# Two 64-row column strips per tile in the experts of a two-layer kernel

## The chip, the cores and the metric

The kernel runs on one core of one Trainium2 chip. The metric is the time of one execution on the device, in microseconds (us); the kernel before takes 3040.6 us, the median of three runs (3038.39 to 3043.71).

Engines are named as in the profile: PE is TensorE's matmul, PEld its weight load, DVE is VectorE, ACT is ScalarE, POOL is GpSimd, SP is SyncE. A "q" behind the name (ACTq, SPq) is the sequencer of that engine, which here issues DMAs.

## The reference

Two layers, each a sequence mixer and a mixture of experts, on 4 x 512 = 2048 tokens of width 512. The change touches the experts of the second layer ("layer 1" in the code). What it computes, cut to what matters:

```python
T, H, E, K, I = 2048, 512, 32, 8, 256
logits = x @ router_w; scores = sigmoid(logits)
# 4 of 8 groups of experts are kept per token, then the best 8 experts
tkw = take_along_axis(scores, top_k_index); tkw = tkw / tkw.sum(-1) * 2.5
flat_idx = top_k_index.reshape(-1); sort_idx = argsort(flat_idx)
xs = repeat(x, K)[sort_idx]                      # 16384 rows, sorted by expert
group_sizes = bincount(flat_idx, length=E)
gate = ragged_dot(xs, w_gate, group_sizes)       # [512 x 256] of each expert
up   = ragged_dot(xs, w_up,   group_sizes)       # [512 x 256]
down = ragged_dot(silu(gate) * up, w_down, group_sizes)   # [256 x 512]
routed = (down[unsort] * tkw).sum(axis=1)        # 8 rows added up per token
out = routed + shared(x)                         # everything in float32
```

## The kernel before

The router stage of layer 1 (`route_stage`, here called with L == 1) counts the rows of each expert, rounds each count up to whole tiles of P = 128 rows, and gives each pair of token and expert a slot in a table in HBM, `slots_in` (`xs1`). It writes each token's normalised row into its 8 slots with indirect DMAs from POOL (line 880), together with a record: the 8 weights, the 8 slot numbers and the token's number. It also writes which expert each tile belongs to (`tile_expert`), and after how many tiles each expert begins (`ends`). The table is zeroed in advance, during the attention stage; a slot that no token took gives a zero row, whose result goes to a spare row of the output.

How many tiles there are is fixed when the program is built, for the worst routing: NTILE1 = (16384 + 32 x 127) // 128 = 159. Tiles past the last expert's rows are computed all the same, with expert 31's weights.

`expert_stage1` then runs over the 159 tiles. It is written for each engine by hand, with semaphores between them, and every engine takes its work in a fixed order:

- **PE**, in round t: `turn_hidden(t-1)` (two 128-column transposes of the hidden rows, tile `e_psh`, line 2032), `up(t)` (four matmuls with the tile's 128 transposed rows as the stationary side and 512 columns of gate and up weights as the moving side, `e_psg`, line 2025), `down(t-1)` (two such matmuls into `e_pso`, line 2041). Each float32 matmul stands in the profile as two MATMUL rows, so `up` is eight rows and `down` four.
- **ACT**: `gate(t)` (SiLU of the gate half, `e_sg`, line 1896), then in two of every four rounds `reload` (one load of records, or four loads of rows, for tiles some rounds ahead, lines 1913 and 1908), then `empty(t-1)` (the result times the row's weight, `e_yo`, line 1903), which waits for `down(t-1)`.
- **DVE**: transposes the rows of tile t+1 (`e_xsT`, line 1960), copies the turned hidden rows of tile t-1 (`e_hT`, line 1965), multiplies gate by up (`e_h`, line 1970), and with four short operations works out the weight and the target row of each slot (`e_mine`, `e_pad`, `e_wrow`, `e_dest`).
- **POOL**: `add(t)`, one indirect DMA per tile that adds the 128 result rows into the output (line 1877). Two such adds must not touch the same row at once. Rows of one expert are of different tokens, so adds of one expert may be in flight together: tiles go by turns to two lanes, each with a semaphore of its own. An add always waits until the one before it in its lane has landed, and where the expert changes it waits for the tile just before it too (the table `after` holds that count). Eight result buffers (OUT = 8) lie between ACT and POOL.
- **SP**: `refill` loads one expert's weights (1.5 MB in three DMAs) into a ring of four, as soon as the expert three before it is done; `announce` tells PE that an expert's weights are there.

Layer 0's experts, which the change doesn't touch, have 64 rows each. They already run two experts side by side: one in the left 64 columns of the PE array, one in the right 64 (`tile_position`, lines 1681 and 1700).

## Time and profile before

| | us |
|---|---|
| median of three runs | 3040.6 |
| the profiled execution | 3042.4 |
| its span, first to last instruction | 3040.7 |
| first matmul of layer 1's experts | 2166.0 |
| last start of an `up` matmul | 3023.6 |
| end of the last result written by ACT (`e_yo`) | 3029.5 |
| last add issued | 3031.2 |

The stage of layer 1's experts is the last of the program, about 875 us of 3041. In the profiled execution PE is busy for 88% of the span, DVE for 48%, POOL for 37%, ACT for 25%; the mean granted clock of PE is 0.956 of full speed. A group of rows gives the line, engine, operation and tiles, the count, the busy time, the mean of one in ns, and behind the last bar how long the engine was idle just before these instructions and what ended the idle time. The 192 ns weight loads of PEld run beside matmuls. A MATMUL row's duration is longer than its share of the engine, since matmuls are pipelined: the spacing of their starts tells what one costs.

### The profile page before, as it was taken

The page shows a single profiled execution, that of the slowest core. Times are in us where ns is not written, and L with a number is a line of the kernel's source. Part 1 is how long each engine was busy: PE and PEld are TensorE (multiplying, and loading weights), DVE is VectorE, ACT ScalarE, POOL GpSimd, SP SyncE. Part 2 cuts the span into 40 slices and gives each one's busy share as a digit, 9 for nine tenths or more (in the row PEclk, how much of TensorE's full clock was granted, in tenths as well). Part 3 has the DMA queues.
Part 4 walks back from the last instruction along what each step waited for, and adds up shares of the span by engine and source line. Part 5 has one row for each costly group of instructions (what it writes and reads, how often), then busy time and mean ns, then how long its engine had stood idle before and what let it go on. Part 6 is the DMA issues. An engine that isn't in the chain of part 4 may idle for free. (4 is left out here: it accounts for less than half of the span.)

```text
span 3040.7 us, 33280 instructions
## 1 busy us (share of the span) xinstructions
PE 2672.1 (88%) x8935; PEld 1175.4 (39%) x8936; DVE 1459.8 (48%) x2609; ACT 773.9 (25%) x1190; POOL 1121.2 (37%) x803
## 2 busy tenths in 40 slices
PE   5888975799999887588999998994499999999998
PEld 2343432344444343233333333441244444444443
DVE  7999999532010033155666564620244444444443
ACT  4747554110000010033333342100011211111111
POOL 2777656233100041126555632257322222232222
PEclk8999999999999999789999998997799999999999
DMA  3333322310300399780177001345677867887765
GB/s 127 112 100 108 81 65 68 115 57 14 117 0 14 116 342 339 247 223 27 41 198 199 12 1 49 133 172 210 159 167 154 179 125 145 181 187 158 157 98 71
DMA packets 364039, 385.31 MB, mean 127 GB/s; under 512 B 69666, under 2 KB 268643, under 8 KB 363938
## 3 DMA queue, kind: packets, MB, share of 16 engines
q1 hardware_dynamic: 212962, 243.49, 25.9%
q0 software_dynamic: 45376, 97.18, 15.4%
q10 hardware_dynamic: 105600, 43.35, 7.2%
q8 instruction: 56, 0.92, 0.1%
q14 instruction: 45, 0.37, 0.0%
HBM read 236.15 MB, written 160.53 MB: 130 GB/s over the span
## 5 line engine op out<-in xcount | busy, mean ns | idle before, releaser
L2025 PE MATMUL e_psg<-e_wgu,e_xsT 128*128 x1272 | 575.0, 595 | 80.5 <-DVE e_xsT L1960 80.5
L1877 POOL DMA_INDIRECT out_x<-e_yo,e_dest x159 | 246.7, 1551 | 629.1 <-DMA out_x<-e_yo,e_dest 343.6
L285 POOL TENSOR_TENSOR hc<-hs,bcst 128x1024 f32<-128x1024 f32 x128 | 300.8, 2350 | 176.6 <-DVE ps_b L505 170.0
L2025 PEld LDWEIGHTS e_psg<-e_wgu,e_xsT 128*128 128x128 f32 x1272 | 231.3, 192 | 311.1 <-issue 311.1
L630 PE MATMUL ps_y<-hc,ident 128*128 128x512 f32 x512 | 241.3, 609 | 90.2 <-POOL hc L285 89.9
L1970 DVE TENSOR_TENSOR e_h<-e_psg,e_sg 128x256 f32<-128x256 f32 x159 | 67.6, 425 | 496.1 <-ACT e_sg L1896 490.1
L2041 PE MATMUL e_pso<-e_wd,e_hT 128*128 x636 | 298.9, 592 | 0.7 <-ACT e_yo L1903 0.7
L511 DVE TENSOR_TENSOR_SCAN hs<-dA,ps_b 128x1024 f32<-128x1024 f32 x128 | 292.6, 2286 | 6.6 <-ACT dA L415 2.4
L1233 PE MATMUL r_ps_t<-r_wd,r_h 128*128 128x512 f32 x480 | 209.6, 597 | 8.5 <-DVE r_h L982 4.3
L1896 ACT ACTIVATE e_sg<-e_psg 128x256 f32<-128x256 f32 x159 | 61.1, 384 | 530.5 <-PE e_psg L2025 530.5
L982 DVE TENSOR_TENSOR r_h<-r_ps_u,r_sg 128x512 f32<-128x512 f32 x60 | 41.4, 691 | 318.1 <-PE r_ps_u L1214 308.8
L415 ACT ACTIVATE dA<-dt,a_neg 128x511 f32<-128x511 f32 x256 | 165.5, 713 | 111.0 <-DVE hs L511 105.9
L2629 DVE TENSOR_REDUCE a_nm<-a_ps 128x2 f32<-128x992 f32 x128 | 146.1, 1185 | 88.7 <-PE a_ps L2873 88.4
L630 PEld LDWEIGHTS ps_y<-hc,ident 128*128 128x128 f32 x512 | 92.8, 191 | 233.2 <-POOL hc L285 138.2
L1960 DVE STREAM_TRANSPOSE e_xsT<-e_xs 128x512 f32<-128x512 f32 x159 | 175.4, 1104 | 11.2 <-DMA e_xs<-slots_in 6.7
L2041 PEld LDWEIGHTS e_pso<-e_wd,e_hT 128*128 128x128 f32 x636 | 120.8, 190 | 152.5 <-issue 152.5
L880 POOL DMA_INDIRECT slots_in<-r_xn,scat x128 | 126.4, 987 | 135.7 <-DMA slots_in<-r_xn,scat 55.0
L1903 ACT ACTIVATE e_yo<-e_pso,e_wrow 128x512 f32<-128x512 f32 x159 | 109.3, 688 | 260.9 <-PE e_pso L2041 172.0
L2391 ACT ACTIVATE a_pt<-a_ps 128x1024 f32<-128x1024 f32 (+1 forms) x128 | 126.2, 1022 | 188.4 <-PE a_ps L2890 127.6
L915 ACT ACTIVATE r_sg<-r_ps_g 128x512 f32<-128x512 f32 x60 | 35.8, 597 | 522.9 <-PE r_ps_g L1214 522.9
L505 DVE TENSOR_TENSOR ps_b<-du,bcst 128x1024 f32<-128x1024 f32 x128 | 159.4, 1246 | 8.4 <-DVE hs L511 0.5
L1214 PE MATMUL r_ps_g<-r_xnT,r_wgu 128*128 128x512 f32 x352 | 158.6, 593 | 0.0
(415 smaller groups left out, 3492.6 us busy)
## 6 DMA issues: line engine op xcount, KB each, us to landing
slots_in<-zeros SPq DMA_DIRECT2D x160, 256.0 KB, 2.3
e_xs<-slots_in ACTq DMA_DIRECT2D x160, 256.0 KB
bcst<-bc_rows SPq DMA_DIRECT2D x128, 256.0 KB, 4.4
e_wgu<-in_wg SPq DMA_DIRECT2D x32, 512.0 KB
e_wgu<-in_wu SPq DMA_DIRECT2D x32, 512.0 KB
e_wd<-in_wd SPq DMA_DIRECT2D x32, 512.0 KB
e_w<-in_wg SPq DMA_DIRECT2D x11, 1408.0 KB
e_w<-in_wu SPq DMA_DIRECT2D x11, 1408.0 KB
```

The costliest lines, as they stand in the source:

```text
L285: pool.tensor_tensor(hc[:, it % 2, half(h), :], hs[:, it % 2, half(h), :], bc(bcst[:, q, 1, :], 1, HB), ALU.mult).then_inc(sem["hc"], 1)
L415: i = act.activation(dA[:, it % 2, t, 1:], dt[:, b % 2, t, 1:], ACT.Exp, scale=a_neg[:, n, t:t + 1])
L505: dve.tensor_tensor(ps_b[:, :, :], du[:, b % 2, half(h), :], bc(bcst[:, q, 0, :], 1, HB), ALU.mult)\
L511: dve.tensor_tensor_scan(hs[:, it % 2, half(h), :].rearrange(flat), dA[:, it % 2, half(h), :].rearrange(flat), ps_b[:, :, :].rearrange(fla ...
L630: i = pe.matmul(ps_y[:, t, :], c["ident"][:, :], hc[:, it % 2, t, :], start=False, stop=False, skip_group_check=True)
L1214: i = pe.matmul(ps[:, f % 2, :], w[:, k, f * P:(f + 1) * P], xnT[:, b, k, :], start=k == 0, stop=k == KH - 1)
L1233: i = pe.matmul(ps_t[:, j % 2, :], h[:, f, j * P:(j + 1) * P], wd[:, f, :], start=f == 0, stop=f == FC - 1)
L1877: pool.indirect_dma_start(out[:, :], bass.IndirectOffsetOnAxis(dest[:, q, 0:1], 0), yo[:, q, :], None, bounds_check=T + 2 * P - 1, oob_is_ ...
L1960: dve.transpose(xsT[:, q % 2, :, :].rearrange("p k (s j) -> p k s j", j=DQ), xs[:, q // RING % 2, part, :].rearrange("p s (i k) -> p k s i ...
L2025: j = pe.matmul(ps_g[:, q % 2, :], xsT[:, q % 2, k, :], wgu[:, bass.ds(e % RING, 1), k, :], start=k == 0, stop=k == KH - 1)
L2041: j = pe.matmul(ps_o[:, q % 2, :], hT[:, q % 2, a, :], wd[:, bass.ds(e % RING, 1), a, :], start=a == 0, stop=a == NW - 1)
L2629: dve.tensor_reduce(nm[:, i % 8, 2 * z:2 * z + 2], ps[:, at:at + 2, 0:S2], AX_X, ALU.max, negate=True)\
```

## The change

Counts are rounded up to HALF = 64 rows per expert instead of 128. A tile still has 128 rows, but is now two strips of 64 rows, and its second strip can belong to another expert than the first. The worst case is 287 strips, so NTILE1 becomes 144.

- **PE** runs each of `up`'s and `down`'s matmuls as two: rows 0 to 63 in the left 64 columns of the array, rows 64 to 127 in the right. The left strip's weights are read from the ring `e_wgu`, `e_wd`, the right strip's from copies, `e_cgu` and `e_cd`. The transposes of the hidden rows stay as they are, over 128 columns.
- **The copies**: ACT copies the second strip's gate and up weights (128 x 2048 float32, 1 MB) for tile t+2 at the end of each round; DVE copies its down weights (128 x 1024) for tile t+1 at the end of each round, after a wait for `down(t-1)`. Both first load the strip's expert number and wait until it is announced. They copy whether or not the two strips have the same expert.
- **POOL** issues two adds per tile, one per strip; the lanes are now the strips. Strip s of tile t waits for strip s of tile t-1 to have landed, and, where the expert changes, for the strip just before it.
- **ACT** also loads the token numbers a second time, into `e_token`, laid out by strips (64 x 8 x 2 words), behind each load of records.
- **SP** announces expert e+3 right behind the refill that loads it, and refills the next only after that.
- In the router, the table of experts is by strips (three columns instead of two), and `ends` is worked out later, as half the strips, rounded up.

```diff
+HALF = P // 2
+NHALF1 = (T * K1 + E * (HALF - 1)) // HALF
+NTILE1 = (NHALF1 + 1) // 2
+NSLOT1 = NTILE1 * P
...
             @block.sync
...
+                for s in range(AHEAD):
+                    announce(s, 0)
                 with sp.Fori(0, E // RING - 1) as i:
                     for q in range(RING):
-                        announce(q, i)
                         refill(i * RING + q, q)
+                        announce((q + AHEAD) % RING, i + (1 if q > 0 else 0))
...
             @block.gpsimd
...
+                    for s in range(2):
...
+                        if before is not None:
+                            hold(pool, out_of[1 - s], before, c["held"])
+                        if not head:
+                            hold(pool, out_of[s], landed_before, c["held"])
...
+                        pool.indirect_dma_start(out[:, :], bass.IndirectOffsetOnAxis(dest[:, q, s:s + 1], 0), yo[half(s), q, :], None,
...
             @block.scalar
...
+                    act.dma_start(token[:, r, :, :], D["xs1"][bass.ds(row0, RING * P), H + 2 * K1:H + RECW + 1]
+                                  .rearrange("(v p) w -> p v w", p=HALF)).then_inc(rec_in[r], 16)
+
+                def copied(t, q):
+
+                    e = act.value_load(ids[0:1, bass.ds(2 * t + 1, 1)], min_val=0, max_val=E - 1)
+                    hold(act, sem["ready"], 1 + e + 1, c["held"])
+                    act.activation(cgu[:, q % 2, :, :], wgu[:, bass.ds(e % RING, 1), :, :].rearrange("p o k n -> p (o k) n"),
+                                   ACT.Copy).then_inc(sem["cgu"], 1)
...
                         gate(i * OUT + q, q)
                         reload(i * OUT + q, q)
                         empty(i * OUT + q - 1, q + OUT - 1)
+                        copied(i * OUT + q + 2, q)
...
             @block.vector
...
+                def copied(t, q):
+
+                    e = dve.value_load(ids[0:1, bass.ds(2 * t + 1, 1)], min_val=0, max_val=E - 1)
+                    hold(dve, sem["ready"], 1 + e + 1, c["held"])
+                    if not (isinstance(t, int) and t < 2):
+                        dve.wait_ge(sem["down"], 1 + t - 1)
+                    dve.tensor_copy(cd[:, q % 2, :, :], wd[:, bass.ds(e % RING, 1), :, :].rearrange("p o k n -> p (o k) n"))\
+                       .then_inc(sem["cd"], 1)
...
                         product(t, q)
                         addressed(t, q, i + 1)
+                        if not (last and q == REST - 1):
+                            copied(t + 1, q + 1)
...
             @block.tensor
...
                     pe.wait_ge(sem["xsT"], 1 + t + 1)
+                    pe.wait_ge(sem["cgu"], 1 + t + 1)
                     for k in range(KH):
-                        j = pe.matmul(ps_g[:, q % 2, :], xsT[:, q % 2, k, :], wgu[:, bass.ds(e % RING, 1), k, :],
-                                      start=k == 0, stop=k == KH - 1)
+                        for s in range(2):
+                            w = cgu[:, q % 2, k, :] if s else wgu[:, bass.ds(e % RING, 1), k, :]
+                            j = pe.matmul(ps_g[half(s), q % 2, :], xsT[:, q % 2, k, half(s)], w, start=k == 0, stop=k == KH - 1,
+                                          tile_position=(0, s * HALF), skip_group_check=True)
```

On PE, one round in the steady loop: the transposes (`e_psh`), `up` (`e_psg`) and the start of `down` (`e_pso`). Before:

```order
L2032 MATMUL e_psh<-ident,e_h 128x128 x2
L2023 REGISTER_ALU
L2025 ISA
L2025 MATMUL e_psg<-e_wgu,e_xsT 128x512
L2025 ISA
L2025 MATMUL e_psg<-e_wgu,e_xsT 128x512
L2025 ISA
L2025 MATMUL e_psg<-e_wgu,e_xsT 128x512
L2025 ISA
L2025 MATMUL e_psg<-e_wgu,e_xsT 128x512
L2036 TENSOR_LOAD e_ids
```

The same place on PE with the change:

```order
L2077 MATMUL e_psh<-ident,e_h 128x128 x2
L2070 ISA
L2070 MATMUL e_psg<-e_wgu,e_xsT 64x512
L2070 MATMUL e_psg<-e_cgu,e_xsT 64x512
L2070 ISA
L2070 MATMUL e_psg<-e_wgu,e_xsT 64x512
L2070 MATMUL e_psg<-e_cgu,e_xsT 64x512
L2070 ISA
L2070 MATMUL e_psg<-e_wgu,e_xsT 64x512
L2070 MATMUL e_psg<-e_cgu,e_xsT 64x512
L2070 ISA
```

Each matmul over 128 rows has become a pair over 64, between transposes that still span 128.

On ACT, the start of the stage: the loads of rows (`e_xs`) and records (`e_rec`) and the first SiLU. Before:

```order
L1908 DMA e_xs<-slots_in 32x16x128 x4
L1913 DMA e_rec<-slots_in 128x4x17
L1908 DMA e_xs<-slots_in 32x16x128 x4
L1913 DMA e_rec<-slots_in 128x4x17
L1896 ACTIVATE e_sg<-e_psg 128x256 x2
```

The same place on ACT with the change:

```order
L1919 DMA e_xs<-slots_in 32x16x128 x4
L1924 DMA e_rec<-slots_in 128x4x17
L1926 DMA e_token<-slots_in 64x8x2
L1919 DMA e_xs<-slots_in 32x16x128 x4
L1924 DMA e_rec<-slots_in 128x4x17
L1926 DMA e_token<-slots_in 64x8x2
L1931 TENSOR_LOAD e_ids
L1931 ISA x2
L75 REGISTER_ALU
L1933 ISA
L1933 ACTIVATE e_cgu<-e_wgu 128x2048
```

Two token loads and then the first weight copy, for which PE's first `up` waits, stand ahead of the first SiLU.

On POOL, the adds of the steady loop. Before, one per tile:

```order
L1871 ISA
L1871 TENSOR_LOAD e_after
L1871 ISA x2
L1877 DMA out_x<-e_yo,e_dest 2304x512
L73 REGISTER_ALU
L1871 ISA
```

The same place on POOL with the change, one tile:

```order
L1881 TENSOR_LOAD e_after
L1881 ISA x2
L75 REGISTER_ALU
L1888 DMA out_x<-e_yo,e_dest 2304x512
L1881 ISA
L1881 TENSOR_LOAD e_after
L1881 ISA x2
L1888 DMA out_x<-e_yo,e_dest 2304x512
```

The second add has a load of its own from `after`, and waits of its own.

## Rows read from the trace of the kernel before

**Rows 1.** The page, groups of layer 1's `up` and adds:
```profile
L2025 PE MATMUL e_psg<-e_wgu,e_xsT 128*128 x1272 | 575.0, 595 | 80.5 <-DVE e_xsT L1960 80.5
L1877 POOL DMA_INDIRECT out_x<-e_yo,e_dest x159 | 246.7, 1551 | 629.1 <-DMA out_x<-e_yo,e_dest 343.6
```

**Rows 2.** Busy time by stretch; columns PE, PEld, DVE, ACT, POOL, clock, DMA share, GB/s:
```profile
2400.00:2600.00 200.00, 200.00 (x522) 93.54 (x521) 82.46 (x261) 40.35 (x75) 57.36 (x37) 1.00 0.76 142
```

**Rows 3.** Timeline, one round in steady state; start, duration, instruction, [idle before <-releaser]:
```profile
2603.87 3.60 PE L2025 MATMUL e_psg<-e_wgu,e_xsT 128*128 x8
...
2607.51 0.38 ACT L1896 ACTIVATE e_sg<-e_psg 128x256 f32<-128x256 f32 x1 [2.84 <-PE e_psg L2025]
...
2607.92 0.42 DVE L1970 TENSOR_TENSOR e_h<-e_psg,e_sg 128x256 f32<-128x256 f32 x1 [3.04 <-ACT e_sg L1896]
...
2609.25 3.60 PE L2025 MATMUL e_psg<-e_wgu,e_xsT 128*128 x8
2609.36 0.69 ACT L1903 ACTIVATE e_yo<-e_pso,e_wrow 128x512 f32<-128x512 f32 x1 [1.47 <-PE e_pso L2041]
```

**Rows 4.** Timeline of layer 0's strips, weight loads of `down` in pairs:
```profile
1128.37 0.14 PEld L1700 LDWEIGHTS e_pso<-e_w,e_hT 128*64 128x64 f32 x2 [0.28 <-issue]
1128.80 0.14 PEld L1700 LDWEIGHTS e_pso<-e_w,e_hT 96*64 96x64 f32 x2 [0.28 <-issue]
```

**Rows 5.** Timeline, layer 0, from 64-column matmuls to 128-column transposes:
```profile
1139.39 0.49 PE L1681 MATMUL e_psu<-e_w,e_xsT 128*64 128x352 f32 x2
1139.81 0.39 PE L1668 MATMUL e_psx<-ident,r_wgu 128*128 128x128 f32 x1
```

**Rows 6.** The transposes of layer 0, all 60: duration ns min/median/max:
```profile
L1668 PE MATMUL e_psx<-ident,r_wgu x60: 283/285/387, 1067.9 to 1255.8; 128*128 128x128 f32 x60
```

**Rows 7.** Timeline, layer 0, from 128-column transposes to 64-column matmuls and their loads:
```profile
1123.22 0.75 PE L1668 MATMUL e_psx<-ident,r_wgu 128*128 128x128 f32 x4
1123.90 1.07 PE L1720 MATMUL e_psa<-x_resid 128*64 128x512 f32 x2
...
1124.38 0.14 PEld L1720 LDWEIGHTS e_psa<-x_resid 128*64 128x64 f32 x1 [0.29 <-issue]
1124.81 0.14 PEld L1720 LDWEIGHTS e_psa<-x_resid 128*64 128x64 f32 x1 [0.29 <-issue]
```

**Rows 8.** ACT groups, from SBUF to SBUF, of two sizes:
```profile
L365 ACT ACTIVATE w<-w 128x512 f32<-128x512 f32 x16 | 9.5, 627 | 6.0 <-DVE e L467 6.0
L2381 ACT ACTIVATE a_sd<-a_sd 128x1024 f32<-128x1024 f32 x4 | 4.2, 1057 | 4.2 <-DVEq L2559 4.2
```

**Rows 9.** Timeline, start of the stage:
```profile
2156.16 2.02 ACTq L1908 DMA_DIRECT2D e_xs<-slots_in  x4
...
2164.09 3.63 ACTq L1913 DMA_DIRECT2D e_rec<-slots_in  x1
...
2166.05 6.33 PE L2025 MATMUL e_psg<-e_wgu,e_xsT 128*128 x8 [80.53 <-DVE e_xsT L1960]
```

**Rows 10.** ACT timeline, the four loads of rows in two rounds:
```profile
2182.75 2.14 ACTq L1908 DMA_DIRECT2D e_xs<-slots_in  x4
...
2785.27 4.68 ACTq L1908 DMA_DIRECT2D e_xs<-slots_in  x4
```

**Rows 11.** POOL timeline, adds at two changes of expert:
```profile
2186.68 1.58 POOL L1877 DMA_INDIRECT out_x<-e_yo,e_dest  x1 [4.45 <-ACT e_yo L1903]
2196.91 1.55 POOL L1877 DMA_INDIRECT out_x<-e_yo,e_dest  x1 [8.65 <-issue]
...
2857.46 1.55 POOL L1877 DMA_INDIRECT out_x<-e_yo,e_dest  x1 [6.66 <-issue]
2863.42 1.55 POOL L1877 DMA_INDIRECT out_x<-e_yo,e_dest  x1 [4.41 <-issue]
```

**Rows 12.** The chain of waits near the end, where no weights load: issue to landing:
```profile
3001.46 4.71 DMA out_x<-e_yo,e_dest
```

**Rows 13.** POOL's scatter of the router, another indirect DMA:
```profile
L880 POOL DMA_INDIRECT slots_in<-r_xn,scat x128 | 126.4, 987 | 135.7 <-DMA slots_in<-r_xn,scat 55.0 <-DVE r_xn L1032 45.6 <-issue 35.1
```

More of the change, by code:

```diff
@@ L125, in constants @@
         idx_i = own("idx_i", [P, E], I32)
-        tile_i = own("tile_i", [P, 2], I32)
+        tile_i = own("tile_i", [P, 3], I32)
         @block.gpsimd
@@ L1128, in _ @@
                     first_slots(base1)
-                    for a in range(2):
+                    for a in range(3):
                         step(dve.tensor_scalar(past[:, :], tcum[:, :], c["tile_no"][:, a:a + 1], None, ALU.is_le))
                         step(dve.tensor_reduce(te[:, a:a + 1], past[:, :], AX_X, ALU.add))
+                    step(dve.tensor_scalar(tf[0:1, :], tcum[0:1, :], 1.0, None, ALU.add))
+                    step(dve.tensor_copy(ti[0:1, :], tf[0:1, :]))
+                    step(dve.tensor_scalar(route["ends"][0:1, 1:], ti[0:1, :], 1, None, ALU.arith_shift_right), wait=False)
                     step(dve.tensor_scalar(te[:, :], te[:, :], float(E - 1), None, ALU.min))
@@ L1804, in expert_stage1 @@
         spare1 = pl.sb("e1_spare1", [P, 2])
-        apart = pl.sb("e1_apart", [1, NTILE1], I32)
-        after_i = pl.sb("e1_afteri", [1, NTILE1 + 1], I32)
-        after = pl.sb("e1_after", [1, NTILE1], I32)
+        apart = pl.sb("e1_apart", [1, 2 * NTILE1], I32)
+        after_i = pl.sb("e1_afteri", [1, 2 * NTILE1], I32)
+        after = pl.sb("e1_after", [1, 2 * NTILE1], I32)
+        token = pl.sb("e1_token", [HALF, 2, RING * 2, 2])
         mine = pl.sb("e1_mine", [P, 2, K1])
         wrow = pl.sb("e1_wrow", [P, OUT, 1])
-        pad = pl.sb("e1_pad", [P, 2, 1])
-        dest = pl.sb("e1_dest", [P, OUT, 1], I32)
+        pad = pl.sb("e1_pad", [HALF, 2, 2])
+        dest = pl.sb("e1_dest", [HALF, OUT, 2], I32)
         ps_g = pl.ps("e1_psg", [P, 2, 512])
@@ L1816, in expert_stage1 @@
                                               "htr", "hT", "down", "yo", "added", "preset", "iota", "named", "chosen", "dest",
-                                              "apart", "after")}
+                                              "apart", "after", "cgu", "cd")}
         landed = [sem[f"w{s}"] for s in range(RING)]
@@ L1861, in _ @@
                 pool.wait_ge(sem["after"], 1 + 1)
                 def add(t, q, turn):
-                    same = 8 * OUT * turn + 16 * (q // 2)
-                    head = isinstance(turn, int) and turn == 0
+                    head = isinstance(turn, int) and turn == 0 and q == 0
+                    landed_before = 16 * OUT * turn + 16 * q
                     hold(pool, sem["yo"], 1 + t + 1, c["held"])
-                    if head and q < 3:
-                        before = 16 if q > 0 else None
-                    else:
-                        before = pool.value_load(after[0:1, bass.ds(t, 1)], min_val=16, max_val=16 * NTILE1)
@@ L1872, in add @@
-                    if before is not None:
-                        hold(pool, out_of[1 - q % 2], before, c["held"])
-                    if not (head and q < 2):
-                        hold(pool, out_of[q % 2], same, c["held"])
-                        pool.sem_inc(sem["added"], 1)
-                    pool.indirect_dma_start(out[:, :], bass.IndirectOffsetOnAxis(dest[:, q, 0:1], 0), yo[:, q, :], None,
-                                            bounds_check=T + 2 * P - 1, oob_is_err=True, compute_op=ALU.add)\
-                        .then_inc(out_of[q % 2], 16)
+                    for s in range(2):
+                        if head and s == 0:
+                            before = None
+                        elif (head and s == 1) or (isinstance(turn, int) and turn == 0 and q == 1 and s == 0):
+                            before = 16
+                        else:
+                            before = pool.value_load(after[0:1, bass.ds(2 * t + s, 1)], min_val=16, max_val=16 * NTILE1)
+                        if before is not None:
+                            hold(pool, out_of[1 - s], before, c["held"])
+                        if not head:
+                            hold(pool, out_of[s], landed_before, c["held"])
+                            if s == 1:
+                                pool.sem_inc(sem["added"], 1)
+                        pool.indirect_dma_start(out[:, :], bass.IndirectOffsetOnAxis(dest[:, q, s:s + 1], 0), yo[half(s), q, :], None,
+                                                bounds_check=T + 2 * P - 1, oob_is_err=True, compute_op=ALU.add)\
+                            .then_inc(out_of[s], 16)
@@ L1985, in addressed @@
                     dve.tensor_reduce(wrow[:, q, :], mine[:, q % 2, :], AX_X, ALU.add).then_inc(sem["chosen"], 1)
[L1986 removed]
+                    dve.scalar_tensor_tensor(out=dest[:, q, :], in0=pad[:, q % 2, :], scalar=-1.0, in1=word,
                                              op0=ALU.add, op1=ALU.add).then_inc(sem["dest"], 1)
@@ L2040, in down @@
                     for a in range(NW):
-                        j = pe.matmul(ps_o[:, q % 2, :], hT[:, q % 2, a, :], wd[:, bass.ds(e % RING, 1), a, :],
-                                      start=a == 0, stop=a == NW - 1)
+                        for s in range(2):
+                            w = cd[:, q % 2, a, :] if s else wd[:, bass.ds(e % RING, 1), a, :]
+                            j = pe.matmul(ps_o[half(s), q % 2, :], hT[:, q % 2, a, half(s)], w, start=a == 0, stop=a == NW - 1,
+                                          tile_position=(0, s * HALF), skip_group_check=True)
                     j.then_inc(sem["down"], 1)
```

73 lines of the change are left out of this document (40 added, 33 removed).

## The prediction

> **What bounds the kernel now.** I read the page first, then the busy time by stretch, then the timeline of one round, and last POOL's adds. Layer 1's experts are the last 875 us, and there PE is the bound: it waits once, 80.5 us, before the stage's first matmul [rows 1], and in a stretch of 200 us it is busy for 200.00 us at the full granted clock (1.00, the 2.4 GHz level) [rows 2]. One round, from `up` to `up`, takes 2609.25 - 2603.87 = 5.38 us [rows 3]. It holds 12 MATMUL rows of 512 columns and two transposes; 159 rounds are 855 us, which is the stage. ACT and DVE are idle for more than half of each round. POOL is not: its 159 adds are busy for 246.7 us and wait for 629.1, over half of it for earlier adds to land [rows 1]. It keeps up, but it is the engine nearest to PE.
>
> **Fewer tiles.** 15 rounds of 5.38 us go: -80.7 us.
>
> **Strips on PE.** Layer 0's experts show what a pair of 64-column matmuls costs. Their weight loads come in pairs, and the pairs stand 1128.80 - 1128.37 = 0.43 us apart [rows 4], for 512 columns. Twelve times 0.43 is 5.16, which leaves 0.22 of a 5.38 us round for two transposes, 0.11 each: so 0.43 is also what one 128-column matmul costs today. Two strips cost what one full matmul costs, and their two loads (0.14 us) fit beside it. Nothing is added there.
>
> What is added is the turn from one width to the other, twice per round: the transposes stay 128 wide. Layer 0 shows both. From 64 to 128: the last pair starts at 1139.39 to 1139.42 and streams 352 columns, 0.43 x 352 / 512 = 0.29 us, so the next could start at 1139.71; it starts at 1139.81, 0.10 late [rows 5], and this first transpose lasts 0.39 us where the median of 60 is 0.285, another 0.10 [rows 5, 6]. From 128 to 64: four transposes span 0.75 us from 1123.22, so the last starts at 1123.22 + 0.75 - 0.285 = 1123.685, and the next matmul 0.215 later instead of the 0.11 that a transpose takes: 0.11 late. The pair after the next is loaded at 1124.38, 0.48 after 1123.90 where 0.43 is the rule (1124.81 - 1124.38): another 0.05 [rows 7]. Sum: 0.20 + 0.16 = 0.36 us per round, so a round takes 5.74 us, and 144 x 0.36 = +51.8 us. The ends: if only the late starts count, 0.21 per round, +30; nothing at all if `up`'s first load could slip in early, +0. No row speaks for more than 0.36. I take 0.36, since both parts are there in one and the same handover.
>
> The Trainium skill, "TensorEngine Tiling (Array Packing)", Key Properties, says that a change of tiling mode drains TensorE. The trace agrees, with the 0.20 and 0.16 us above. Who goes only by that page's promise of independent tiles would leave the 51.8 us out and expect about 2970 us.
>
> **ACT's copy.** SBUF to SBUF, 128x512 takes 627 ns and 128x1024 takes 1057 [rows 8]: 430 ns per 512 columns, so 128x2048 takes 627 + 3 x 430 = 1917 ns. In a plain round `e_yo` starts 2609.36 - 2607.51 = 1.85 us after `e_sg` and ends at 2.54 [rows 3]. Then come the load of the expert's number, a wait that is met, and the copy. What number and waits cost before the engine starts is not shown for ACT; POOL does the like between the last `e_yo` (3029.5) and the last add (3031.2), 1.7 us, and zero is the other end. The copy ends at 4.5 to 6.2 us. The next `e_sg` is due at 5.74, and PE needs its product later still: `e_h` ends at 2608.34 and PE's transposes start at 2609.25 - 0.22 = 2609.03, a cover of 0.7 us [rows 3]. So a plain round is free. In one round of four the loads of rows hold ACT for 2.14 us first [rows 10], `e_yo` ends near 3.1 and the copy at 5.0 to 6.7: at most 0.3 late beyond the cover, 36 x 0.3 = 11 us, at least nothing. Once in a while these loads take 4.68 us [rows 10]; then the copy ends near 8 and PE loses about 2 us. I take +3 us in all, range 0 to 11. Behind the copy on ACT stand the next SiLU and the next loads; DVE and PE wait for the SiLU.
>
> **DVE's copy** of 128x1024 waits for `down(t-1)`, which ends when `e_yo` starts, at 1.85. ACT's 1057 ns for the same size is the nearest row. With the row transposes (1.1) and the hidden copy (0.4) behind it, which are queued behind this wait, DVE is done at 4.4; `down` needs the hidden rows at about 5.4, and the next product begins at 6.1. Hidden; a copy twice as long would just still be.
>
> **Start of the stage.** PE's first `up` now waits for the first copy, which stands behind ten loads of before and two new ones. ACT was done with its loads at 2164.09 + 3.63 = 2167.72, and PE started at 2166.05 [rows 9]. A new token load costs between 0.5 (a load of rows here, 2.02 / 4) and 3.6 us (the record load just before, when the queue is full) [rows 9]; one of each kind gives 4.1, the copy 1.9 more: 2167.7 + 4.1 + 1.9 = 2173.7 at worst, 2170.6 with both loads cheap. +4.6 to +7.7; I take +6. The later copies have a whole slow first `up` (6.33 us) as cover.
>
> **Weights.** `ready` is now announced before it is needed by two tiles more, and SP holds each refill until the one before it has landed. With the reference's routing the experts take 273 strips; in its tightest place (expert 16, 3 strips) expert 19 must land within two rounds, 11.5 us, for 1.5 MB. Once, 0 to 5 us: +1.
>
> **Router, zeroing, end.** Three more short DVE operations come after the first slots are out and beside 128 scatters of POOL; fewer slots are zeroed in a stretch where the DMA queues idle: 0. At the end two half adds stand for one: one more issue, less to land: 0, range -1 to +2.
>
> **Sum** against the profiled execution, 3042.4: -80.7 + 51.8 + 3 + 6 + 1 = -18.9, so 3023.5. The median of before is 1.8 under its profiled execution: **3022 us**.
>
> **The rivals.**
>
> *A, the chain of adds becomes the bound (slower).* Today's add has two rounds, 10.8 us, from its issue to the next in its lane. After the change each lane has one add per round, 5.74 us. A quiet full add lands in 4.71 us [rows 12], and where the next waits for it, it goes out after 2863.42 - 2857.46 = 5.96; a busy one, with weights on their way, after 10.23 [rows 11]. A half add should be shorter: its issue perhaps 0.99 us, as the router's scatter, instead of 1.55 [rows 1, 13], and some of the transfer goes. Bounds for the quiet cycle: 5.96 - 0.56 = 5.4 if only the issue shrinks, (5.96 - 0.56) / 2 = 2.7 if all the rest halves; I take 4.5. Busy: 9.7 to 4.8, I take 7.9. How many adds are busy no row tells; with 28% as an estimate, a lane needs 0.72 x 4.5 + 0.28 x 7.9 = 5.45 us on average: just under 5.74. Of the 31 changes of expert 12 fall inside a tile, by that same routing, and put its second strip some 4 us back, 48 us in all; the result buffers let POOL fall seven rounds behind, 40 us, and the spare 0.29 us per round gives back 42 over the stage. So it holds. At the full add's figures the mean is 0.72 x 5.4 + 0.28 x 9.7 = 6.6: 0.86 us more than PE per round, over the 118 rounds with weights on their way 101 us, plus 48, less the 40 in the buffers: +109, some 3131 us. At a mean of 6.0, nearer to my figures, it is 31 + 48 - 40 = +39: **3061 us**. The point from which it decides is a mean cycle of about 5.7 us. Against it: nothing in today's POOL rows shows it falling behind for more than one add; for it: over half of its waits are for landings already.
>
> *B, ACT becomes the bound.* If numbers, waits and copy take 1.5 us more than taken, every fourth round is 1.2 us longer than the cover allows, 36 x 1.2 = +43, and plain rounds lose a little: 3066 us, slower too. Against it: ACT has only 0.38 + 0.69 us of work per round today.
>
> *C, the turns of width are hidden.* Then -51.8 falls off: 2970 us. Against it: both handovers of layer 0 show the delay, in both halves.
>
> **How the numbers follow.** Forecast 0.60 (its own range 3008 to 3035), A 0.22, B 0.08, C 0.10. A measurement of this kernel tells 0.2% from no change, 6 us: faster is below 3034.5. The forecast's upper edge and mild cases of A and B lie within 0.2% either way: same 0.08. Faster 0.67, slower 0.25. For 8 in 10 the range leaves out the deeper half of C and the dear half of A: 2985 to 3070.
>
> **What would show it.** PE rows of `up` and `down`: 144 x 16 and 144 x 8, pairs 0.43 us apart; the first transpose of a round near 0.39 us, the rest 0.28; a round of 5.74 us. PE's wait before the first `up` some 86 us and for ACT's copy. POOL adds x288 near 1 us each; their start stays within about 20 us of `e_yo`'s end if the forecast is right. If A is right, ACT's `e_yo` waits for POOL's adds in groups, and PE for `e_yo`. If B is right, PE's transposes wait for `e_h` behind copies on ACT. A round of 5.4 us would be C. The prediction is wrong if a half add's landing isn't shorter than a full one's, or if the copy takes much over 2 us.

## The result: 3080 us, slower by 38

The changed kernel takes 3079.95 us (3074.26 to 3085.48), the kernel before beside it 3042.15 us (3038.39 to 3047.17): a ratio of 1.0123, 95% interval 1.0096 to 1.0150. The forecast was 3022 us. Among the experiments, one execution of chain32 (3674 us) and one of apart_out (3615 us) ran at a clearly lower granted clock, 0.81 and 0.735, and the ratios leave these two out.

Of the profiled execution (span 3083.8 us), the chain of waits by line and four groups of the page:

```profile
DMA out_x<-e_yo,e_dest 22%; POOLq L1881 1%; PE e_psg L2070 0%; ACTq L1919 0%; POOL out_x L1888 0%; POOLq L76 0%; POOLq L1888 0%; POOLq L75 0%; ACTq L1926 0%; ACT e_yo L1914 0%; ACT e_cgu L1933 0%; PE e_pso L2089 0%; ACTq L1924 0%; POOLq L1887 0%; POOLq L1894 0%
...
L1888 POOL DMA_INDIRECT out_x<-e_yo,e_dest x288 | 424.9, 1475 | 489.9 <-DMA out_x<-e_yo,e_dest 262.4
L2070 PE MATMUL e_psg<-e_wgu,e_xsT 128*64 x1152 | 529.0, 602 | 80.9 <-ACT e_cgu L1933 80.9
...
L1933 ACT ACTIVATE e_cgu<-e_wgu 128x2048 f32 x144 | 275.2, 1912 | 133.2 <-issue 131.2
...
L2007 DVE COPY e_cd<-e_wd 128x1024 f32 x144 | 105.6, 733 | 132.0 <-PE e_pso L2089 84.6
```

The chain that ended last no longer runs through PE's matmuls: 22% of the span is the landing of adds, where in the kernel before 27% were PE's matmuls. Busy time by stretch, columns as in [rows 2], and one round of PE's timeline:

```profile
2250.00:2400.00 150.00, 150.00 (x684) 50.96 (x682) 79.01 (x210) 77.99 (x79) 72.53 (x49) 1.00 0.71 146
2400.00:2600.00 200.00, 194.47 (x866) 64.36 (x864) 99.00 (x264) 98.55 (x100) 96.05 (x65) 0.98 0.67 136
2600.00:2800.00 200.00, 179.82 (x792) 59.03 (x788) 91.08 (x245) 89.97 (x92) 88.09 (x60) 0.97 0.70 150
```

```profile
2602.63 0.64 PE L2070 MATMUL e_psg<-e_wgu,e_xsT 128*64 x1
...
2607.93 0.50 PE L2077 MATMUL e_psh<-ident,e_h 128*128 128x128 f32 x2
2608.37 0.64 PE L2070 MATMUL e_psg<-e_wgu,e_xsT 128*64 x1
```

A round that nothing holds up takes 5.74 us, as forecast. Up to 2400 us PE is busy throughout, as in [rows 2]; after that it loses 6 and then 20 us in 200. Who waits, between 2400 and 3000 us (in total, times, longest):

```profile
POOL out_x L1888 <- DMA out_x<-e_yo,e_dest: 168.0, 77, 5.8
...
DVE e_mine L2018 <- POOLq L1887: 74.2, 44, 10.8
...
PE e_pso L2089 <- DVE e_hT L1994: 33.3, 19, 8.6
```

POOL waits for adds to land. DVE, which may fill a buffer's addresses only after that buffer's add of eight tiles ago has landed (`added`, L1887), stands for POOL in `e_mine`; the hidden rows' copy `e_hT` stands behind it on DVE, and PE waits for that. How far POOL is behind shows in the counts of a stretch that begins with the stage and ends at 2500 us:

```profile
L1888 POOL DMA_INDIRECT out_x<-e_yo,e_dest x96 | 142.3, 1483 | 195.5 <-DMA out_x<-e_yo,e_dest 103.2 <-issue 53.4 <-ACT e_yo L1914 39.0
L1914 ACT ACTIVATE e_yo<-e_pso,e_wrow 128x512 f32<-128x512 f32 x53 | 36.4, 687 | 89.5 <-PE e_pso L2089 68.6 <-issue 8.7 <-DVE e_dest L2025 6.7
```

96 half adds are 48 tiles, of 53 finished ones. In the kernel before the same stretch has 60 of each.

**Where the 43 us between the two profiled spans went.** Four moments of the changed kernel's timeline: the first load of rows, the first and the last SiLU, the last add.

```profile
2160.63 2.65 ACTq L1919 DMA_DIRECT2D e_xs<-slots_in  x4
...
2183.49 0.38 ACT L1907 ACTIVATE e_sg<-e_psg 128x256 f32<-128x256 f32 x1 [4.62 <-PE e_psg L2070]
...
3050.91 0.38 ACT L1907 ACTIVATE e_sg<-e_psg 128x256 f32<-128x256 f32 x1 [3.33 <-PE e_psg L2070]
...
3075.08 1.42 POOL L1888 DMA_INDIRECT out_x<-e_yo,e_dest  x1 [1.20 <-DMA out_x<-e_yo,e_dest]
```

and of the kernel before, the first and last SiLU (its first load is in [rows 9]):

```profile
2172.41 0.38 ACT L1896 ACTIVATE e_sg<-e_psg 128x256 f32<-128x256 f32 x1 [104.55 <-PE e_psg L2025]
...
3024.24 0.38 ACT L1896 ACTIVATE e_sg<-e_psg 128x256 f32<-128x256 f32 x1 [2.97 <-PE e_psg L2025]
```

- The stage begins 2160.63 - 2156.16 = 4.5 us later. No reading speaks for the change as the cause: the experiments, most of them with its router, begin the stage anywhere from 2149 to 2159 us. So below I give the **stage's length** too, from the first load of rows to the end of the span: 884.5 us before, 923.2 after.
- First load to first SiLU: 16.25 us before, 22.86 after, +6.6.
- First to last SiLU: before 851.8 us, of which 158 x 5.38 = 850.0; after 867.4 us, of which 143 x 5.74 = 820.8. The rounds give 29.2 us back, and 46.6 - 1.8 = 44.8 us are stalls.
- Last SiLU to the end: 16.5 us before, 32.9 after, +16.4: POOL still has its backlog to add.

Sum: 4.5 + 6.6 - 29.2 + 44.8 + 16.4 = 43.1 us.

### The profile page after: what moved, and what is told of

Read it like the earlier page. It is cut to its first block and busy times, and to the rows that moved or that the text cites. A ratio compares the mean times of both kernels' runs of the same rounds, so it can differ in the third digit from the quotient of the medians.

```text
span 3083.8 us, 39087 instructions
## 1 busy us (share of the span) xinstructions
PE 2665.0 (86%) x10451; PEld 1058.0 (34%) x10454; DVE 1541.4 (50%) x2653; ACT 1032.3 (33%) x1305; POOL 1298.6 (42%) x932
## 5 line engine op out<-in xcount | busy, mean ns | idle before, releaser
L1888 POOL DMA_INDIRECT out_x<-e_yo,e_dest x288 | 424.9, 1475 | 489.9 <-DMA out_x<-e_yo,e_dest 262.4
L2070 PE MATMUL e_psg<-e_wgu,e_xsT 128*64 x1152 | 529.0, 602 | 80.9 <-ACT e_cgu L1933 80.9
L2070 PE MATMUL e_psg<-e_cgu,e_xsT 128*64 128x512 f32 x1152 | 529.0, 602 | 0.0
L1933 ACT ACTIVATE e_cgu<-e_wgu 128x2048 f32 x144 | 275.2, 1912 | 133.2 <-issue 131.2
L2089 PE MATMUL e_pso<-e_wd,e_hT 128*64 x576 | 278.1, 606 | 34.2 <-DVE e_hT L1994 34.0
L2089 PE MATMUL e_pso<-e_cd,e_hT 128*64 128x512 f32 x576 | 278.3, 606 | 0.0
L2070 PEld LDWEIGHTS e_psg<-e_wgu,e_xsT 128*64 128x64 f32 x1152 | 146.9, 137 | 349.1 <-issue 332.2
L1914 ACT ACTIVATE e_yo<-e_pso,e_wrow 128x512 f32<-128x512 f32 x144 | 99.0, 687 | 277.5 <-PE e_pso L2089 205.9
L2007 DVE COPY e_cd<-e_wd 128x1024 f32 x144 | 105.6, 733 | 132.0 <-PE e_pso L2089 84.6
L1989 DVE STREAM_TRANSPOSE e_xsT<-e_xs 128x512 f32<-128x512 f32 x144 | 167.6, 1164 | 6.5 <-DMA e_xs<-slots_in 6.5
```

Of the source, the lines that this page charges most:

```text
L1888: pool.indirect_dma_start(out[:, :], bass.IndirectOffsetOnAxis(dest[:, q, s:s + 1], 0), yo[half(s), q, :], None, bounds_check=T + 2 * P - ...
L1933: act.activation(cgu[:, q % 2, :, :], wgu[:, bass.ds(e % RING, 1), :, :].rearrange("p o k n -> p (o k) n"), ACT.Copy).then_inc(sem["cgu"], 1)
L1989: dve.transpose(xsT[:, q % 2, :, :].rearrange("p k (s j) -> p k s j", j=DQ), xs[:, q // RING % 2, part, :].rearrange("p s (i k) -> p k s i ...
L2070: j = pe.matmul(ps_g[half(s), q % 2, :], xsT[:, q % 2, k, half(s)], w, start=k == 0, stop=k == KH - 1, tile_position=(0, s * HALF), skip_g ...
L2089: j = pe.matmul(ps_o[half(s), q % 2, :], hT[:, q % 2, a, half(s)], w, start=a == 0, stop=a == NW - 1, tile_position=(0, s * HALF), skip_gr ...
```

## The experiments

| kernel | us | ratio to before (95%) | stage's length, us |
|---|---|---|---|
| before | 3042.15 | 1 | 884.5 |
| changed | 3079.95 | 1.0123 (1.0096 to 1.0150) | 923.2 |
| one_add | 3015.73 | 0.9919 (0.9901 to 0.9936) | 861.2 |
| narrow_turn | 3078.06 | 1.0124 (1.0103 to 1.0145) | 920.9 |
| one_add_narrow | 2999.20 | 0.9866 (0.9849 to 0.9882) | 847.8 |
| four_lanes | 3019.69 | 0.9934 (0.9914 to 0.9954) | 863.0 |
| split_before | 3138.73 | 1.0326 (1.0302 to 1.0349) | 987.0 |
| strips_before | 3096.90 | 1.0191 (1.0167 to 1.0214) | 939.9 |
| early | 3072.14 | 1.0112 (1.0090 to 1.0134) | 912.3 |
| best | 2996.66 | 0.9859 (0.9831 to 0.9886) | 840.2 |
| chain128 | 3251.53 | 1.0699 (1.0668 to 1.0730) | |
| chain64 | 3634.86 | 1.1960 (1.1925 to 1.1995) | |
| chain32 | 3502 and 3674 | | |
| lone64 | 3012.25 | 0.9911 (0.9894 to 0.9927) | 857.0 |
| apart_out | 3016.24 | 0.9921 (0.9900 to 0.9943) | 860.4 |
| apart_wait | 3078.76 | 1.0119 (1.0101 to 1.0137) | 927.1 |

**Is it the adds? one_add.** One 128-row add per tile; two only where two experts meet in a tile, the second after the first has landed. `put` issues the add.

```diff
-                    for s in range(2):
...
+                    pool.reg_load(two, mixed[0:1, bass.ds(t, 1)])
+                    with pool.If(two):
+                        put(q, slice(0, HALF), first)
...
+                        hold(pool, first, landed_first, c["held"])
+                        put(q, slice(HALF, P), out_of[q % 2], dest2)
+                    with pool.Else():
+                        put(q, slice(0, P), out_of[q % 2])
```

> The changed kernel with one 128-row add per tile on two lanes by turns, as in the kernel before; only a tile whose two strips belong to different experts takes a branch on POOL with two 64-row adds, the second after the first has landed. Everything else, the turns of width and the copies too, stays. Theory 1 (each of the two lanes has one add per round, and what a lane needs for one, 6.15 us on average, is more than the round's 5.73 us): a 128-row add has two rounds again, so the stalls summed over the rounds (47 us) and most of what POOL has left at the end (some 13 us) go: 3080 - 60 = 3020 us, POOL's start stays within about 10 us of the end of e_yo. Theory 2 (PE waits for something else that the change added, ACT's or DVE's copies or the weights): the adds matter for the end only, 3065 us or more.

3015.73 us: 64 us less, and PE is busy without a gap where it lost 26 us in 400:

```profile
2400.00:2600.00 200.00, 200.00 (x910) 68.06 (x910) 107.36 (x345) 104.00 (x105) 58.80 (x38) 1.00 0.67 130
2600.00:2800.00 200.00, 200.00 (x910) 67.88 (x908) 107.90 (x350) 103.48 (x105) 57.56 (x38) 1.00 0.83 181
```

Copies, strips and weights are all still there, so none of them makes the stalls by itself. This is also what the forecast's own terms give: 884.5 - 28.9 (tiles and turns) + 6.6 (start) = 862 us of stage, and 861.2 came. So its +3 for ACT's copy and +1 for the weights were nothing that shows.

**Does a faster PE help? narrow_turn and one_add_narrow.** The turn of the hidden rows in 64 columns, first with the half adds, then with the single ones.

```diff
-                        j = pe.transpose(ps_h[:, q % 2, a * P:(a + 1) * P], h[:, q % 2, a:F1:NW], c["ident"][:, :])
+                        for s in range(2):
+                            j = pe.matmul(ps_h[half(s), q % 2, a * P:(a + 1) * P],
+                                          h[:, q % 2, a + s * HALF * NW:(s + 1) * HALF * NW:NW], c["ident"][:, :],
+                                          start=True, stop=True, tile_position=(0, s * HALF), skip_group_check=True)
```

> The changed kernel with each 128-column transpose of the hidden rows made as two 64-column matmuls against the identity, one in each column strip, so that PE never changes its width inside a round; the adds stay two 64-row ones per tile. A round that nothing holds up should take 5.38 us instead of 5.73. Theory 1 (the lanes of adds are the bound): POOL can't use the faster rounds, the buffers are full earlier, and the time stays at 3065 to 3082 us. Theory 2 (PE's path sets the time, with stalls of another cause): 144 x 0.36 = 52 us less, 3028 us.

> Both edits at once, the single adds and the 64-column turns of the hidden rows. Theory 1: with the adds out of the way PE is the bound and its round is 5.38 us: 3020 - 52 = 2968 us. Theory 2: what holds PE up now is neither, and the time stays over 3010 us.

3078.06 us: with the half adds, nothing. 2999.20 us with single adds: 16.5 us less than one_add, where 52 were expected. One round of one_add_narrow shows why:

```profile
2603.87 0.61 PE L2111 MATMUL e_psh<-ident,e_h 128*64 128x128 f32 x8
...
2604.30 0.59 PE L2103 MATMUL e_psg<-e_wgu,e_xsT 128*64 x1
```

The turn now takes 0.43 us, in eight rows, where two transposes took 0.22: a matmul against the identity stands there twice for each product, a transpose once. 0.36 saved and 0.21 paid leaves 0.15 per round (two rounds of it start 5.59 us apart), 22 us over the stage; 16.5 came. The delay of changing width is gone; I had overlooked the price of its replacement.

**Landing or issuing? four_lanes.** As many half adds, but two rounds for each to land; at a change of expert POOL waits for every other lane.

```diff
-        out_of = [pl.sem0(f"e1_out{lane}") for lane in range(2)]
+        out_of = [pl.sem0(f"e1_out{lane}") for lane in range(4)]
...
+                        lane = q % 2 * 2 + s
```

> The changed kernel with its 288 adds of 64 rows kept, but on four lanes instead of two (a lane for each strip of every second tile), so that an add has two rounds to land before the next on its lane; at a change of expert POOL waits for all lanes. POOL issues as many adds as before. Theory 1 (a lane's time from one add to the next is the bound): as one_add, 3020 to 3030 us. Rival (POOL's own issuing, 288 x 1.48 us with the waits and register work between them, is the bound): POOL stays behind, 3060 us or more.

3019.69 us. POOL issues its 288 adds (415.3 us busy) and keeps up. Issuing isn't the bound, though a half add's issue takes 1.42 to 1.50 us on average, by the run, and not the 0.99 that I took.

**Each part alone on the kernel before: split_before and strips_before.**

```diff
+                    for s in range(2):
...
+                            hold(pool, out_of[1 - s], before, c["held"])
...
+                            hold(pool, out_of[s], gone, c["held"])
...
+                        pool.indirect_dma_start(out[:, :], bass.IndirectOffsetOnAxis(dest[0:HALF, q, s:s + 1], 0),
+                                                yo[s * HALF:(s + 1) * HALF, q, :], None,
```

> The kernel before (159 tiles of 128 rows, no strips, no copies, no second set of weights), with one part of the change alone: each tile's add is made as two adds of 64 rows, one on each of the two lanes, with their own token numbers loaded. Theory 1 (a lane needs about 6.1 us from one 64-row add to the next, and has one per round): the round is 5.38 us here, so POOL loses about 0.7 us per round, the eight buffers are full by about the 55th tile, and then the adds set the pace: 159 x 6.1 = 970 us from the first add at about 2180, some 3145 us; with an expert's change never inside a tile a lane may need only 5.7, and then 3085. So 3080 to 3150 us. Rival (half adds are slow only because of the copies or the weights of the changed kernel): within 15 us of the kernel before, 3042 to 3057 us.

```diff
-                        j = pe.matmul(ps_g[:, q % 2, :], xsT[:, q % 2, k, :], wgu[:, bass.ds(e % RING, 1), k, :],
+                        for s in range(2):
+                            j = pe.matmul(ps_g[s * 64:(s + 1) * 64, q % 2, :], xsT[:, q % 2, k, s * 64:(s + 1) * 64],
+                                          fixed[:, k, :] if s else wgu[:, bass.ds(e % RING, 1), k, :], start=k == 0, stop=k == KH - 1,
```

> The kernel before with every 128-column matmul of layer 1's experts made as two 64-column ones in the two column strips; the second strip reads a fixed buffer that is filled once, instead of the expert's weights, so the output of half the rows is not the reference's. Adds, tiles and turns of the hidden rows stay. It prices the turn between widths alone: 0.36 us for each of 159 rounds, a round of 5.74 us, 3042 + 57 = 3099 us. If a change of width cost nothing, 3042 us. The adds keep up here (two rounds for each).

3138.73 us and 3096.90 us. The half adds cost the old kernel 99 us by their ratio, with no strip or copy in it. The strips cost it 58 us where 57 were forecast: its first `up` matmuls stand at 2603.65 and 2609.39, 5.74 us apart. No tile of the kernel before has two experts, so in split_before all 31 changes of expert fall between tiles. Its first and its last add:

```profile
2177.87 1.51 POOL L1879 DMA_INDIRECT out_x<-e_yo,e_dest  x1 [23.65 <-ACT e_yo L1924]
...
3128.63 1.42 POOL L1879 DMA_INDIRECT out_x<-e_yo,e_dest  x1 [1.34 <-DMA out_x<-e_yo,e_dest]
```

950.76 us for 317 steps is 6.00 us per tile and lane. For the changed kernel it is (3075.08 - 2191.82) x 2 / 287 = 6.155 us, over its 5.74.

**What does one add cost alone? chain128, chain64, chain32.** All adds one after the other on one lane: chain128 with one 128-row add per tile (two half adds in the 12 tiles with two experts), chain64 with all 288 half adds, chain32 with the first 32 rows of each strip alone, so that half of the results are left out. The cut is of chain64 and chain32.

```diff
-                            hold(pool, out_of[1 - s], before, c["held"])
...
-                            hold(pool, out_of[s], landed_before, c["held"])
+                            hold(pool, out_of[0], 32 * OUT * turn + 32 * q + 16 * s, c["held"])
...
-                            .then_inc(out_of[s], 16)
+                            .then_inc(out_of[0], 16)
```

> The changed kernel with all adds on one lane, one after the other: a 128-row add per unmixed tile and two 64-row ones in each of the 12 mixed ones, 156 in all. Once the buffers are full the whole stage goes at the pace of one add from its issue to the next, so the time divided by the number of adds is the price of an add. From the quiet 5.96 us and the busy 10.23 us that the kernel before showed at changes of expert I expect 6.2 to 7 us each: 2180 + 156 x 6.2 to 7 = 3147 to 3272 us. It can be read only if it is over the 5.73 us of a round.

> The changed kernel with its 288 adds of 64 rows on one lane, one after the other. Theory a (an add costs mostly the same whatever its rows: its issue 1.48 us and a landing that hardly shrinks): 5.0 to 5.8 us each, 2180 + 288 x 5.0 to 5.8 = 3620 to 3850 us. Theory b (only the two lanes side by side make a half add slow; alone it costs what the prediction took, 4.5 us when quiet, or half of a full add's): 3.7 to 4.6 us each, 3245 to 3505 us.

> As the run of 64-row adds on one lane, but each add takes only the first 32 rows of its strip, so half of the results are left out of the output. Theory a: nearly the time of 64-row adds, within 10% of the cost of each (4.6 to 5.6 us, 3500 to 3790 us). If the landing goes with the rows, an add costs 1.5 us less than the 64-row one or more, some 3.7 us or under, 3245 us or less.

First to last add by the number of steps: (3239.22 - 2189.35) / 155 = 6.77 us, (3624.03 - 2184.04) / 287 = 5.02 us, (3493.87 - 2184.52) / 287 = 4.56 us. Halving the rows takes off 1.75 us, halving again 0.46: a half add costs three quarters of a full one, not half. (24 of chain128's 156 adds are half ones; with those taken out at 5.02, a full add is 7.1 us, an estimate.) Both times lie within reading a's, at the cheap edge; but the step from 128 to 64 rows is no small one, so "mostly the same whatever its rows" goes too far. These slower stages spread the weights over more time, so with PE's full pace an add may cost somewhat more. But 5.02 is well under 5.74: why then 6.155 with two lanes?

**The other lane: lone64, apart_out, apart_wait.** lone64 has the first strips' adds alone; apart_out keeps both lanes but sends the second's adds elsewhere, so that nothing need wait at a change of expert; apart_wait sends them elsewhere and waits all the same.

```diff
-                            hold(pool, out_of[1 - s], before, c["held"])
...
-                        pool.indirect_dma_start(out[:, :], bass.IndirectOffsetOnAxis(dest[:, q, s:s + 1], 0), yo[half(s), q, :], None,
+                        pool.indirect_dma_start((D["x0"] if s else out)[:, :], bass.IndirectOffsetOnAxis(dest[:, q, s:s + 1], 0),
```

> The changed kernel with the first strip's adds alone: one 64-row add per tile, all on one lane, one per round; the second strip's adds are left out, so the output lacks them. Tiles, copies, weights and the pace of PE stay, so an add meets the same traffic of weights as in the changed kernel, which it doesn't in the slower runs with all adds on one lane. Theory 1a (a lane by itself gets on with some 5.3 us per add; two lanes get to 6.1 because POOL issues for both in one order, so that each waits for the slower of the two, and at mixed tiles one waits for the other): one lane keeps up with the 5.73 us of a round and nothing stalls, 3018 to 3026 us, with POOL's start within about 15 us of e_yo's end. Theory 1b (a 64-row add itself takes over 5.73 us on average with weights on their way): the stalls stay, 3050 to 3075 us.

> The changed kernel with its 288 half adds on two lanes, in the same order on POOL, but the second strips' adds go to another buffer in HBM (that of the layer before, which nothing reads any more), so the output lacks them. Since the two lanes then never touch the same row, no lane has to wait for the other at a change of expert, and those waits are gone; a lane still waits for its own add before. Theory E (each of the 31 changes of expert costs the chain some 2.5 to 3 us, because at most one add of each lane is on its way and POOL stands until both have landed): 31 x 2.6 = 80 us less in the chain of adds, which brings a lane from 6.15 us to about 5.6, under the round's 5.73, and the stalls and the late end go: 3016 to 3026 us. Theory O (POOL's one order over two lanes is what costs): the lane stays at about 6.0 us, 3055 to 3080 us.

> The control of the run before: the second strips' adds go to the same other buffer (the output lacks them), but POOL keeps all its waits at changes of expert. If the destination itself matters for nothing, the time is that of the changed kernel, 3070 to 3082 us, and the difference between the two runs is the price of the waits alone, under either theory. If adds to one buffer disturb each other, it is faster than 3065 us.

3012.25, 3016.24 and 3078.76 us. The waits for the other lane are worth 3078.76 - 3016.24 = 62.5 us, about what one_add gained; POOL's single order over two lanes, my reading 1a, costs nothing that can be seen. The destination matters for nothing. (apart_out also lacks POOL's loads from `after`, one per add; but four_lanes has a load per add and keeps up, and where nothing is waited for, the next add goes out 0.30 us behind the last with or without them.) Four adds of POOL's timeline, strips 78 to 81, in the changed kernel and then in apart_out. Strip 80 is the first of tile 40 and begins a new expert:

```profile
2447.78 1.42 POOL L1888 DMA_INDIRECT out_x<-e_yo,e_dest  x1 [1.80 <-DMA out_x<-e_yo,e_dest]
2449.50 1.55 POOL L1888 DMA_INDIRECT out_x<-e_yo,e_dest  x1 [0.30 <-issue]
2456.73 1.42 POOL L1888 DMA_INDIRECT out_x<-e_yo,e_dest  x1 [5.69 <-issue]
2458.46 1.55 POOL L1888 DMA_INDIRECT out_x<-e_yo,e_dest  x1 [0.31 <-issue]
```

```profile
2411.98 1.41 POOL L1878 DMA_INDIRECT out_x<-e_yo,e_dest  x1 [1.97 <-DMA out_x<-e_yo,e_dest]
2415.42 1.42 POOL L1878 DMA_INDIRECT x_after<-e_yo,e_dest  x1 [2.03 <-DMA x_after<-e_yo,e_dest]
2417.14 1.55 POOL L1878 DMA_INDIRECT out_x<-e_yo,e_dest  x1 [0.30 <-issue]
2421.06 1.42 POOL L1878 DMA_INDIRECT x_after<-e_yo,e_dest  x1 [2.37 <-DMA x_after<-e_yo,e_dest]
```

and the changed kernel's chain of waits, from the issue of strip 79's add to its landing:

```profile
2449.50 6.20 DMA out_x<-e_yo,e_dest
```

Without the wait strip 80's add goes out 1.72 us after strip 79's. With it 7.23 us pass, POOL idle for 5.69 of them, until the add that it has just issued is down, and both lanes are empty. Not every change shows it so plainly: at strip 73 apart_out too lets 6.69 us pass, waiting for the add before it on its own lane. Over all 31 changes, the add that begins an expert goes out 5.55 us after the one before it in the changed kernel, 5.71 in apart_wait and 3.42 in apart_out; all other adds 2.8 in each. The 19 changes between tiles cost what the 12 inside a tile do: 5.48 and 5.66 us. To bring 143 rounds from 5.74 to 6.155 us takes 59 us, 1.9 us for each of the 31 changes of expert; they cost at least that, since without the waits a lane keeps up with 5.74 and may be faster.

**The start: early and best.** ACT's first copy right behind the first four loads; best has this, the single adds and the 64-column turn.

```diff
-                for r in range(2):
-                    load_rows(r * RING * P, r)
-                    load_rec(r * RING * P, r)
+                load_rows(0, 0)
                 act.wait_ge(sem["ids"], 1 + 16)
                 copied(0, 0)
+                load_rec(0, 0)
                 copied(1, 1)
+                load_rows(RING * P, 1)
+                load_rec(RING * P, 1)
```

> The changed kernel with another order on ACT at the stage's start alone: the first four loads of rows, then the first copy of weights, then the other loads and the second copy. In the changed kernel the first copy starts 14.5 us after the first load and the first SiLU comes 22.9 us after it; here the copy should start after 4 to 6 us and the SiLU come after 17 us or so, as in the kernel before (16.2). Theory 1 says that the adds form one chain from the first to the last, so what the start gains reaches the end, unless the buffers eat it: 5 us less, 3075 us (3071 to 3080).

> One add per unmixed tile, 64-column turns of the hidden rows, and the early first copy together: 2999 us of the two edits, less 5 to 6 us of the start: 2993 us. If the start's gain is hidden behind the first weights or rows, 2999 us.

3072.14 us; the interval overlaps the changed kernel's. By the traces the first SiLU comes 14.4 us after the first load (2154.29 to 2168.66), not 22.9, and the stage is 10.9 us shorter, so the chain of adds does hand the gain on to the end. best takes 2996.66 us, between my two readings, 1.4% less than the kernel before by its ratio, the fastest of all; its interval overlaps one_add_narrow's, its stage is 7.6 us shorter. Both beat the two kernels of this case.

## Why the prediction was wrong

- **Fewer tiles, strips, turns of width: right.** 5.74 us per round in the trace, and +58 us for the turns alone on the kernel before, where 57 were forecast.
- **ACT's and DVE's copies: right.** 1912 ns for 1917 forecast, hidden; DVE's copy 733 ns where 1057 was taken as nearest. Rival B never came near.
- **Start: right.** +6.6 us for +6. PE waited 80.9 us before its first matmul, for ACT's copy; the 86 that I had named stood on the stage's arrival, which varies.
- **End: wrong.** "0, range -1 to +2" was +16.4 us. It held only if POOL had no backlog.
- **The chain of adds: the step that failed.** The forecast held that POOL keeps up, by this sum: 48 us for changes of expert, less 42 of spare time, less 40 in the buffers, so nothing. The opposite stood as rival A, at 0.22 and 3061 us. A half add's issue was taken as 0.99 us, the router's scatter [rows 13]; it is 1.475. The quiet cycle of 4.5 us came out all the same (the three adds behind one another on one lane, every second row):

```profile
2461.19 1.42 POOL L1888 DMA_INDIRECT out_x<-e_yo,e_dest  x1 [1.18 <-DMA out_x<-e_yo,e_dest]
2463.15 1.42 POOL L1888 DMA_INDIRECT out_x<-e_yo,e_dest  x1 [0.54 <-issue]
2465.72 1.41 POOL L1888 DMA_INDIRECT out_x<-e_yo,e_dest  x1 [1.16 <-DMA out_x<-e_yo,e_dest]
2467.70 1.42 POOL L1888 DMA_INDIRECT out_x<-e_yo,e_dest  x1 [0.57 <-issue]
2470.17 1.74 POOL L1888 DMA_INDIRECT out_x<-e_yo,e_dest  x1 [1.06 <-DMA out_x<-e_yo,e_dest]
```

And one lane alone keeps up (lone64), as it would at the mean of 5.45; but lone64 goes at PE's pace and shows only that the mean is no more than 5.74. What was mis-sized is the price of changes of expert: "12 fall inside a tile, 48 us in all". All 31 count. Before, a change cost POOL up to 8.65 us of standing too [rows 11], but each lane had two rounds, 10.8 us, to make it up. With one round per lane, the spare time of a round, 0.29 us by the forecast, is all there is to make up with, whether the change falls inside a tile or between two. The 19 changes between tiles were left out of the sum; at the 4 us that I had put on the 12, 31 changes are 124 us, and the sum would have been +42 or, without the buffers, +82: A would have been the forecast. 61 came (stalls and end).
- **The 40 us in the buffers were no credit.** Buffers let PE run ahead of POOL, but the kernel ends with POOL's last add. From the first add to the last are 883.3 us; 143 rounds of 5.74 are 820.8. The 62 us between them come out in full, as 44.8 us of stalls and 16.4 at the end. By the forecast's own figures, too, 48 against 42 left POOL behind.
- **Not settled: how much of it is the changes and how much the spare.** In the changed kernel the 62 lane cycles (from an add to the next on its lane) in which a change falls average 7.85 us, the other 224 5.68. Read straight, the changes cost 31 x 2.17 = 67 us and not 48, and the spare is 0.06 us a round and not 0.29. But in apart_out, without those waits, the same cycles average 6.50 and 5.51, so the adds around a change are slower for another reason too. It may be the weights that load then; no run tried that. Shown is the sum: without the waits the stalls and the late end are gone.
- **"Nothing in today's POOL rows shows it falling behind for more than one add" was the wrong question.** Those rows were of lanes with twice the time. That over half of POOL's waits were for landings was the sign.
- Of the places named to look at: the round and PE's wait for the copy were as forecast, POOL's adds near 1 us were not, and DVE's wait for `added` with PE behind it was rival A's.

## What to carry to other kernels

When a transfer is split in two and each half gets its own lane, each lane gets an add in every round instead of every second one, so it has half the time for it: compare the time from issue to issue of one lane, waits for other lanes included, with the round, and not the engine's busy share. Count every event that empties all lanes, not only the new ones, and don't subtract what the buffers hold when the kernel ends with the adds. If rows only have to be kept apart at rare borders, split at the borders alone: 156 adds instead of 288 made the same change 0.8% faster than the kernel before instead of 1.2% slower.

## What the runs showed of the hardware

- An indirect accumulating DMA costs POOL nearly the same whatever its rows: 1551 ns for 128 [rows 1], 1415 (split_before) to 1498 (chain64) for 64, 1439 for 32 (chain32). Issue to next issue with all adds on one lane is 6.77, 5.02 and 4.56 us (chain128, chain64, chain32).
- DVE's row transposes (`e_xsT`, 128x512) slowed from 1104 ns on average to 1164 in the changed kernel, whose copies run beside them. Whether the copies do it, and which, was not tried.
- With PE waiting in every round, the granted clock fell. In chain64, between 2400 and 2600 us, PE is busy for 139.78 of 200 us and the mean granted clock is 0.85, so part of the stretch ran at the lower level, 1.2 GHz; in one_add's row above it is 1.00, the 2.4 GHz level:

```profile
2400.00:2600.00 200.00, 139.78 (x518) 40.58 (x516) 56.86 (x160) 59.30 (x60) 59.91 (x41) 0.85 0.46 93
```

- The stage begins between 2149 and 2161 us in these executions, also among kernels with the same code ahead of it (2149.0 in one_add_narrow, 2158.6 in best). Which stage this comes from stays open.
